# A gated delta rule on one core: the first level's small products in two parts around a chain product, and the output norm's denominator as bias of four ScalarE roots

## What is computed

```python
q = l2norm(q) / sqrt(128);  k = l2norm(k);  beta = 2 * sigmoid(x @ Wb)
g = -exp(A_log) * softplus(x @ Wa + dt_bias)
def step(state, inp):
    q_t, k_t, v_t, b_t, g_t = inp
    state = state * exp(g_t)
    for j in range(2):
        kj = k_t[:, j]
        u = (v_t[:, j] - kj @ state) * b_t[:, j]
        state = state + outer(kj, u)
    return state, q_t @ state
o = o * rsqrt(mean(o * o, axis=-1) + 1e-5)          # the output norm
out = (o * norm_w * silu(x @ Wg)) @ Wo
```

## Time and profile before

| | |
|---|---|
| three runs | 4096.15, 4109.01, 4117.0 us; median 4109.01 |
| the profiled execution | 4109.43 us, span 4107.6 us |
| busy share of the span | TensorE 93%, its weight loads 77%, VectorE 68%, ScalarE 54%, GpSimd 38% |
| output norm, first and last turn | 181.6 and 2238.1 us |
| mean granted TensorE clock | 0.97 |

### The profile page before, as it was taken

How to read it: one execution, slowest core, us unless ns; L and a number is a source line. 1 busy time by engine, 2 the same in 40 slices (tenths; PEclk the granted TensorE clock), 3 DMA queues, 4 the chain that set the end, 5 groups by cost and what they waited for, 6 DMA issues and landing times. The chain is left out here.

```text
span 4107.6 us, 108406 instructions
## 1 busy us (share of the span) xinstructions
PE 3812.3 (93%) x38395; PEld 3174.9 (77%) x38395; DVE 2793.9 (68%) x7247; ACT 2233.8 (54%) x6182; POOL 1581.2 (38%) x2837
## 2 busy tenths in 40 slices
PE   6699999999999999999996899699999999999889
PEld 5588877788878888788885788577777877777678
DVE  5577777777777777777773544567777676676564
ACT  2466666666666666666662443344444444444354
POOL 0577677677776677677761000000000000000010
PEclk9999999999999999999996999899999999999999
DMA  4333333333333333333332321211111111110010
GB/s 171 116 87 87 109 94 101 86 91 110 94 97 87 98 109 87 107 94 104 86 98 73 126 75 37 89 44 42 56 40 51 39 56 35 56 56 29 28 62 31
DMA packets 543245, 322.36 MB, mean 78 GB/s; under 512 B 251744, under 2 KB 501088, under 8 KB 541024
## 3 DMA queue, kind: packets, MB, share of 16 engines
q1 hardware_dynamic: 542688, 315.21, 26.5%
HBM read 231.00 MB, written 84.01 MB: 77 GB/s over the span
## 5 line engine op out<-in xcount | busy, mean ns | idle before, releaser
L1038 DVE SCALAR_TENSOR_TENSOR g_conv<-g_r,g_taps,g_conv 128x511 f32<-128x511 f32 (+2 forms) x961 | 713.9, 743 | 28.2 <-issue 9.0
L2070 ACT ACTIVATE a_pr<-a_pr,a_low 128x128 f32<-128x128 f32 (+3 forms) x512 | 286.6, 560 | 391.3 <-DVE a_low L2215 374.5
L2370 POOL TENSOR_TENSOR a_dg<-a_const,a_fl 128x384 fp32r<-128x384 f32 x32 | 26.4, 827 | 1151.8 <-DVE a_fl L2222 1151.8
L2215 DVE CUSTOM_DVE_ANT_0 a_pr<-a_sc,a_bias 128x128 f32<-128x128 f32 (+3 forms) x512 | 242.2, 486 | 192.7 <-issue 172.8
L604 PE MATMUL g_r<-g_x_hi,g_w_hi 128*128 128x512 f32 x646 | 317.4, 491 | 10.0 <-issue 9.3
L901 ACT ACTIVATE g_us<-g_chn 128x128 f32<-128x128 f32 x528 | 146.4, 277 | 299.3 <-PE g_chn L710 296.1
L1898 PE MATMUL a_out<-a_pt,a_v 128*128 128x512 f32 (+3 forms) x1024 | 297.3, 433 | 0.9 <-DVE a_oT L2235 0.9
L1224 POOL TENSOR_TENSOR g_prod<-g_small 64x14 f32<-64x14 f32 (+6 forms) x896 | 227.3, 254 | 151.1 <-DMA g_small<-lower_d 85.8
L1226 POOL TENSOR_TENSOR g_small<-g_small,g_prod 64x14 f32<-64x14 f32 (+6 forms) x896 | 241.2, 269 | 70.3
L1066 DVE SCALAR_TENSOR_TENSOR g_R<-g_chn,g_ctab,g_bv 128x128 f32<-128x128 f32 x462 | 161.1, 349 | 154.4 <-PE g_chn L703 142.5
L1898 PEld LDWEIGHTS a_out<-a_pt,a_v 128*128 128x128 f32 x1024 | 184.7, 190 | 102.6 <-issue 62.2
(11 more groups left out here) (378 smaller groups left out, 11506.3 us busy)
## 6 DMA issues: line engine op xcount, KB each, us to landing
g_w_raw<-w_heads SPq DMA_DIRECT2D x66, 768.0 KB, 4.4
lower_d<-g_L SPq DMA_DIRECT2D x64, 512.0 KB, 3.6
g_U<-upp_d SPq DMA_DIRECT2D x64, 512.0 KB, 5.1
a_w<-w_groups SPq DMA_DIRECT2D x32, 640.0 KB, 4.5
oT_d<-g_oT SPq DMA_DIRECT2D x67, 256.0 KB, 5.0
g_T<-low_d SPq DMA_DIRECT2D x64, 256.0 KB, 3.0
g_T<-low_d SPq DMA_DIRECT2D x128, 128.0 KB, 3.4
f_oT<-oT_d SPq DMA_DIRECT2D x8, 2048.0 KB, 8.4
```

The lines of the kernel that those rows point to most:

```text
L1038: ins = V.scalar_tensor_tensor(out=y[:, k:L], in0=x[:, 0:L - k], scalar=tap, in1=y[:, k:L], op0=ALU.mult, op1=ALU.add)
L2070: A(pr[g % 2][:, i, 0:width(i)], pr[g % 2][:, i, 0:width(i)], ACT.Exp, scale=-1.0, bias=low[g % 2][:, i:i + 1], accum_out=tot[g % 2][:, i: ...
L2215: V.tensor_tensor_reduce(pr[g % 2][:, i, 0:width(i)], sc[i % 2][:, 0:width(i)], bias[tp_][:, i, 0:width(i)], -SCALE, 3.0e38, ALU.add, ALU. ...
```

## The change

`un_small` keeps its first loop; the second one becomes `turn_small`, which TensorE now issues after `chain_s` of step 5. VectorE does `chain_S` of step 5 before it waits for the small products, so all four quarters of `add_small` come after it. The instruction that made `g_oden` is gone with its semaphore; ScalarE waits for its own squares and takes four roots of one column each, with scale 1/128 and the column of `g_qden` as bias.

```diff
--- before.py
+++ after.py
@@ -442,7 +442,7 @@
         R = sb("g_R", [P, P])
         us = sb("g_us", [P, P])
         osq = sb("g_osq", [P, TT, P])
-        oss, oden, osd, orec = (sb(f"g_{n}", [P, TT]) for n in ("oss", "oden", "osd", "orec"))
+        oss, osd, orec = (sb(f"g_{n}", [P, TT]) for n in ("oss", "osd", "orec"))
         on = sb("g_on", [P, TT, P])
         oT = sb("g_oT", [P, L])
         small = sb("g_small", [NSM, SM, SM])
@@ -642,6 +642,9 @@
                         for i, at_ in enumerate(QUAD):
                             h = QUAD[home(i, c)]
                             M.matmul(lev[at_, c % 2, p, SM:2 * SM], T[h, c, at_], nu0[h, c, SM:2 * SM], start=True, stop=True)
+
+            def turn_small(u):
+
                 for p in range(HC):
                     for c in (2 * p, 2 * p + 1):
                         for i in (0, 2):
@@ -806,6 +809,8 @@
                 if inverse:
                     un_small(u)
                 chain_s(u, q, 5, made)
+                if inverse:
+                    turn_small(u)
                 if own:
                     pe.wait_ge(s["d_conv"], 5 * u + 6)
                     spread_end(u + 1)
@@ -1001,8 +1006,10 @@
                 for m in range(TT):
                     ins = A(osq[:, m, :], ob[:, m, :], ACT.Square, accum_out=oss[:, m:m + 1])
                 ins.then_inc(s["d_osq"], 1)
-                act.wait_ge(s["d_oden"], u + 1)
-                A(osd[:], oden[:], ACT.Sqrt).then_inc(s["d_osd"], 1)
+                act.wait_ge(s["d_osq"], u + 1)
+                for m in range(TT):
+                    ins = A(osd[:, m:m + 1], oss[:, m:m + 1], ACT.Sqrt, scale=1.0 / P, bias=qden[(q + 2) % QN][:, m:m + 1])
+                ins.then_inc(s["d_osd"], 1)
                 if own:
                     first_tap(u + 1, 1 - par, K1)
 
@@ -1139,11 +1146,10 @@
                     dve.wait_ge(s["d_kq"], u + 1)
                     dve.wait_ge(s["d_dp"], 2 * u + 1)
                     V.tensor_tensor(own_half(at[q]), pairs(by_chunk(kq_b, C)), pairs(dmt[par][:]), ALU.mult).then_inc(s["d_at"], 1)
+                chain_S(u, q, 5)
                 if inverse:
                     dve.wait_ge(s["d_un"], NLV * u + 1)
                     add_small(u, o, (1, 3))
-                chain_S(u, q, 5)
-                if inverse:
                     dve.wait_ge(s["d_Tc"], 2 * u + 1)
                     add_small(u, o, (0, 2)).then_inc(s["d_U"], 1)
                 chain_R(u, q, 6)
@@ -1161,8 +1167,6 @@
                     ch.link(V.tensor_tensor(bk[:], rk[:], tab[par][:, 0, :], ALU.mult))
                     values(0)
                     values(1)
-                dve.wait_ge(s["d_osq"], u + 1)
-                V.scalar_tensor_tensor(out=oden[:], in0=oss[:], scalar=1.0 / P, in1=qden[(q + 2) % QN][:], op0=ALU.mult, op1=ALU.add).then_inc(s["d_oden"], 1)
                 dve.wait_ge(s["d_osd"], u + 1)
                 ch.link(V.reciprocal(orec[:], osd[:]))
                 V.tensor_tensor(on[:], ob[:], orec[:].unsqueeze(2).to_broadcast([P, TT, P]), ALU.mult).then_inc(s["d_on"], 1)
@@ -1272,7 +1276,7 @@
           "d_proj", "d_tap", "d_rep", "d_gm", "d_dm", "d_exp", "d_conv", "d_silu", "d_gate", "d_ktr", "d_ksq", "d_rk2", "d_rk",
           "d_qtr", "d_qsq", "d_vtr", "d_bv", "d_kq", "d_at", "d_gram", "d_L", "d_dp",
           "d_kend", "d_qg", "d_nu", "d_nus", "d_un", "d_U", "d_Tc",
-          "d_ks", "d_R", "d_u", "d_us", "d_ds", "d_S", "d_o", "d_osq", "d_oden", "d_osd", "d_on", "d_ot", "d_oT", "d_dve"]
+          "d_ks", "d_R", "d_u", "d_us", "d_ds", "d_S", "d_o", "d_osq", "d_osd", "d_on", "d_ot", "d_oT", "d_dve"]
 
 
 def feed_forward(nc, io, sems, p, src, dst, delta_out):
```

## The result

| | runs | median, us | ratio to before, 95% interval |
|---|---|---|---|
| before | 4 | 4111.56 (4096.15 to 4117.0) | |
| changed | 4 | 4161.98 (4154.26 to 4169.1) | 1.0134 [1.0108, 1.0161] |

What follows compares the result with a forecast made beforehand. TensorE's own queue and what it waits for were taken to bound the kernel. Terms +52 - 17 + 13 = +48 us, some +50 with the last, unfilled turn, gave 4159 us from 4109, range 4115 to 4200.

Steps and rivals of the forecast that it cites:

- The ordinary turn: One undisturbed turn of the delta-rule loop, output transposes to output transposes: 31.5 to 31.6 us instead of 30.3.
- the 0.83: Delay in us per turn of chain step 6, through ScalarE's late copy_small, table load, Exp and copy of `g_us`.
- The wait for `g_us`: Sign: TensorE waits some 0.3 to 0.4 us for `g_us` before chain step 6.
- Rival 1: Late table load does not hold chain step 6; moved products cost only their switches: +16, 4125 us, chance 0.17.
- It is worth nothing: Putting chain_S ahead of the additions: S is ready sooner, but chain_ks comes after two spread matmuls in TensorE's queue.
- The stalls (-17 us): TensorE's late-instruction stalls at L650 go, 8.1 us times 2.6, less 4: -17 us (-8 to -29).
- Rival 2: Instruction supply was the true cost; stalls at L644 and L650 both end: faster, middle 4080 us, chance 0.08.
- Part two (+13 us): Four roots replace `g_oden` at the turn's end: +30 us on the path, -17 of stretching saved, net +13.
- Rival 3: Clock falls in ordinary turns, after new waits between small products; every second turn, +76: 4235 us, chance 0.09.
- The drain: Skill's extra some 1380 ns at a table switch; Exp 1.36 us later, turn loses 2.2 us, some 4244 us.
- Rival 4: ScalarE needs a 1.28 us gap between late table load and Exp; turn loses 2.1 us, 4237 us, chance 0.02.
- Part one: Second group of small products moved behind chain step 5, delaying step 6: 63 turns x 0.83 = +52 us.

Runs made afterwards that it cites:

- split_only: Kernel before with only the second group of small products moved behind chain step 5, denominator and root as before: 4164.05 us, ratio 1.0118.
- roots_only: Kernel before with only the denominator instruction replaced by four one-column roots on ScalarE, products in the old order: 4132.15 us, ratio 1.0051.

## Why the prediction was right, point by point

**The ordinary turn** was forecast at 31.5 to 31.6 us and is 31.56. The shift of the second part (1.01), the delay of step 6 (0.82 for 0.83), the roots (0.85) and the way from square to reciprocal (0.91 for 0.92) are all as worked out from the rows. `split_only` and `roots_only` show the two halves of it apart: 0.81 and 0.46 us.

**The limb was only half named.** The prediction put the 0.83 on ScalarE's queue and said that VectorE is late "but less". That is so by 0.14 us. It gave `chain_u` a start near 1350.65, 21.85 us into the turn, and did not ask what then follows; it starts at 22.05 and by itself brings step 6 to 22.88. So the 0.82 is made of 0.32 for the switches, 0.35 for R and 0.14 for the load and the Exp. ScalarE's limb does end last, and its length was right, so nothing of the sum changes. The lesson does: without its table load the change would still have cost 0.68 us a turn. The kernel before had no wait at `chain_u`, and its `g_us` was copied 0.49 us behind it (1350.67 less 1350.18), as without the load (1368.44 less 1367.94 is 0.50), so a load taken away there would have gained nothing either.

**The wait for `g_us`**, said to be 0.3 to 0.4 us, is 0.24, and it stands at the weight load of step 6; that it stands there at all was one of the signs. Rival 1 did not happen: not even with the load taken away is the delay down to its 0.32 of switches.

**"It is worth nothing" was wrong** for the state's new place. I had asked what it gains in the old order, where the small products are early. Behind a late second part, the old place costs 0.40 us of waiting in `chain_ks` and 0.18 us of the turn.

**The stalls (-17 us)** had the right sign. The idle time at L650 and step 5 fell from 9.6 us to 1.4. For its price I compare excesses, without the stretching of `g_oden`: 61.2, 60.0 and 71.2 us with the old order of the small products, 40.0, 55.2, 50.0, 58.1 and 52.5 with the new one. The means differ by 64 - 51 = 13 us, and single profiles by more than that. So the term stands at -13 with an uncertainty of about 10, and a factor of 13 / 8.2 = 1.6 in place of 2.6. Another thing is inside this difference and works against it: `g_bk` took 12.0 to 14.4 us in all in the three old-order kernels and 15.1 to 25.7 in the five with the new order. The prediction had no such term. Rival 2 needed the stalls at L644 to end, and they did not.

**Part two (+13 us)** measured -14 and +32, so +18, beside the late second part. The two terms were +30 and -17. Alone it showed +21.

**The clock** did not fall in ordinary turns: their granted clock is 1.00, at the level of 2.4 GHz, and the 62 turns' mean is 0.99 in one profile and 0.98 in the other, against 0.98 before. Rival 3 did not happen.

**The drain** that was weighed against the trace does not show here. The Exp again starts 1.30 us behind the start of its load, ahead of the 2.66 us that the Trainium skill gives (ScalarE: Activation LUTs, section What ACT_TABLE_LOAD costs), and taking the whole load away gained 0.14 us a turn, as the other limb ends right before it. Rival 4 falls with the 1.30 us.

**Sum.** Part one's ordinary turn measured 0.81 us more (`split_only`), 0.81 x 64 = +52. With the other terms that is +52 - 13 + 18 = +57, against +50 and +56 in two sessions. The forecast's +48 for 64 turns was 2 to 8 us low, inside what two profiles of one kernel differ by. The largest term was right by its mechanism. The two smaller ones were off by 4 and 5 us the same way; that the first session's total came out within 3 us of the forecast all the same is partly chance.

## What to carry to other kernels

When a signal is moved later, follow it on every engine that waits for it down to the next product that needs both, and note how far apart the limbs end: here removing the culprit of the trace would have bought a sixth of the delay. An instruction split into four because its operand must be one column costs its fixed time four times; if it stands on the path, compare that with the hand-off that it saves (0.55 us against 0.09 here). And look at the longest case of a small instruction beside its mean: the 16.8 us that the change wanted were to be had by placing one operand in PSUM.

## What the runs showed of the hardware

- A VectorE instruction of 128x4 elements with both inputs in SBUF took 165 ns at the median and up to 4227 ns. All 18 that took more than 230 ns ended 19 to 24 ns after a GpSimd instruction (the earlier trace rows shows the longest), and that longest one lasted through several GpSimd instructions in a row, of 0.84 to 1.27 us each; with one input in PSUM, 66 of 66 took 161 to 163 ns. The Trainium skill (SBUF — State Buffer, section SBUF: two separate sides) says that such an instruction reads its second input through the port pair of GpSimd and waits until a GpSimd instruction that reads SBUF has let it go; the runs agree, show that the instruction's size is no protection, and that the wait can outlast a single GpSimd instruction.
- TensorE stood idle for up to 1.2 us within runs of 32x32 products with nothing to wait for. Moving the stream by 64 instructions moved these stalls to other lines and turns at the same total time. A stall of 3.1 to 3.6 us at the end of each loop body of 16 turns did not move.
- Two profiles of the same kernel differ by 15 us (changed) and 24 us (part one alone) over 62 turns of which the ordinary ones agree to 0.01 us. What decides how often a stall is followed by a lower clock stays open.
